# Gathered rows of a mixture-of-experts kernel as fp16 halves, transposed by DMA instead of on TensorE

## The reference, cut to what matters

```python
x = x + tanh(g_xattn) * xattn(layernorm(x), ctx, Wq, Wkv_expand, Wout)
xf = layernorm(x)                              # 2048 tokens x 512
scores = softmax(xf @ gate_w.T); weights, idx = top_k(scores, 2)
h = einsum('td,eid->eti', xf, w1)              # 512 -> 256, each expert
g = silu(h) * einsum('td,eid->eti', xf, w3)
eo = einsum('eti,edi->etd', g, w2)             # 256 -> 512
y = sum over the two chosen experts of weight * eo
z = silu(xf @ ws1.T) * (xf @ ws3.T) @ ws2.T    # shared expert
out = x + tanh(g_ffn) * (y + z)
```

## Time and profile before

| | |
|---|---|
| median of 3 runs | 523.39 us (520.7 to 524.97) |
| the profiled execution | 525.32 us |
| its span in the profile | 523.5 us |
| mean granted TensorE clock | 0.947 |
| batches, to the first gather | 0 to 316.7 us |
| tiles of the experts | 316.7 to 523.5 us |

### The profile page before, as it was taken

One profiled execution on the slowest core, in us unless ns is written; L12 is line 12 of the kernel. 1 busy time (PEld: TensorE's weight loads), 2 busy tenths in 40 slices (PEclk: granted clock), 3 DMA queues, 4 the chain that ended last, 5 costly groups with the idle time before them and its releaser, 6 DMA issues. The chain is left out here.

```text
span 523.5 us, 8113 instructions
## 1 busy us (share of the span) xinstructions
PE 435.4 (83%) x2432; PEld 233.2 (45%) x2433; DVE 322.2 (62%) x641; ACT 246.0 (47%) x425; POOL 240.2 (46%) x185
## 2 busy tenths in 40 slices
PE   2699699988999889987756723999999999999991
PEld 1355455554555545544323311454555455455540
DVE  4798768887588865898888952343434343434330
ACT  4877554563356534486733611333433444333430
POOL 4008235405544154466583633255455455555532
PEclk9999789999999999999895975999999999999996
DMA  8970001120011100325649554166666665756652
GB/s 310 418 307 1 0 1 41 41 81 2 1 60 42 60 0 0 117 105 180 242 121 258 131 113 112 30 108 115 120 104 104 114 120 87 123 112 104 121 75 42
DMA packets 26375, 55.31 MB, mean 106 GB/s; under 512 B 9136, under 2 KB 9264, under 8 KB 25712
## 3 DMA queue, kind: packets, MB, share of 16 engines
q0 software_dynamic: 9760, 20.49, 22.2%
q1 hardware_dynamic: 16592, 34.54, 20.3%
HBM read 31.51 MB, written 23.50 MB: 105 GB/s over the span
## 5 line engine op out<-in xcount | busy, mean ns | idle before, releaser
L1288 PE MATMUL bank<-arena 128*128 128x512 f16 (+1 forms) x576 | 111.0, 350 | 3.2 <-issue 1.5
L1288 PE MATMUL bank<-arena,GT 128*128 x468 | 109.2, 384 | 0.2 <-issue 0.2
L521 POOL DMA_INDIRECT out<-Y,entry x39 | 61.6, 1579 | 84.0 <-ACT Y L787 41.1
L1288 PE MATMUL bank<-arena,gT 128*128 (+1 forms) x330 | 81.3, 383 | 5.4 <-DVE gT L810 4.9
L1288 PEld LDWEIGHTS bank<-arena 128*128 128x128 f16 x576 | 56.3, 99 | 52.6 <-issue 5.8
L536 ACT ACTIVATE arena<-bank 128x512 f16<-128x512 f32 (+1 forms) x88 | 49.8, 586 | 50.9 <-PE bank L1288 31.3
L1288 PEld LDWEIGHTS bank<-arena,GT 128*128 128x128 f16 x468 | 46.3, 99 | 48.3 <-issue 2.9
L810 DVE TENSOR_TENSOR GT<-bank,GT 128x512 f16<-128x512 f32 x39 | 27.0, 692 | 61.0 <-ACT GT L536 61.0
L452 POOL TENSOR_TENSOR arena<-arena,rd 128x1024 f32<-128x1024 f32 x16 | 30.5, 1905 | 52.3 <-DVE rd L923 52.3
L1288 PEld LDWEIGHTS bank<-arena,gT 128*128 128x128 f16 x330 | 32.1, 98 | 42.3 <-DVE gT L810 4.6
L1252 DVE SCALAR_TENSOR_TENSOR uu<-th,bank 128x256 f32<-128x256 f32 x39 | 16.4, 421 | 55.8 <-ACT th L772 55.8
(11 more groups left out here) (126 smaller groups left out, 602.2 us busy)
## 6 DMA issues: line engine op xcount, KB each, us to landing
x_sb<-in_experts SPq DMA_DIRECT2D x16, 768.0 KB, 6.0
xrows<-xn SPq DMA_DIRECT2D x16, 256.0 KB, 2.1
out<-x_sb SPq DMA_DIRECT2D x16, 256.0 KB, 2.2
xrows<-Y SPq DMA_DIRECT2D x1, 2304.0 KB, 24.5
out<-Y SPq DMA_DIRECT2D x1, 2304.0 KB, 28.6
x_sb<-in_x SPq DMA_DIRECT2D x2, 1024.0 KB, 9.1
x_sb<-in_x SPq DMA_DIRECT2D x1, 2048.0 KB, 16.4
arena<-in_wq SPq DMA_DIRECT2D x1, 1024.0 KB, 9.3
```

What stands on the lines that cost most here:

```text
L521: nc.gpsimd.indirect_dma_start(out=out, out_offset=bass.IndirectOffsetOnAxis(ap=entry[:, j, 0:1], axis=0), in_=Y[:, j % RING, :], in_offse ...
L1288: last = nc.tensor.matmul(dst, a, b, start=n == 0, stop=n == len(steps) - 1)
```

## The change

`xrows` holds each row as 1024 fp16: 512 high halves and 512 low halves (the same 2 KB). `row_half` makes them before the store: the high one on ACT, the low one on POOL for the batches 0 to 2 and on DVE for the last. Both lie in `xnh`, in the space of `Y` and a part of `G`. The gathered tile of 128 x 1024 fp16 is transposed from `G` to `GT` by one DMA that SP issues (`dma_start_transpose`); the four PE transposes and the `rows_hi` and `rows_lo` of each tile are gone. Gathers run up to five tiles ahead, PE makes the hidden products two tiles ahead, and `gT` has three buffers. The router's and the shared expert's input of the batches is still turned on PE.

```diff
-        xrows = nc.dram_tensor("xrows", (ROWS, D), F32)
+        xrows = nc.dram_tensor("xrows", (ROWS, 2 * D), F16)
...
             def store_rows(b):
                 for i in range(PER):
-                    sp.wait_ge(xn2_ready, 4 * b + i + 1)
+                    sp.wait_ge(row_lo, 4 * b + i + 1)
...
             load_pieces(0, 2)
+            store_rows(B - 2)
             store_base(B - 2, 0, 1)
             load_pieces(2, 4)
             store_base(B - 2, 1, PER)
             sp.wait_ge(st_base, 16 * PER * (B - 1))
-            load_pieces(4, 12)
+            load_pieces(4, 15)
             store_rows(B - 1)
-            load_pieces(12, 15)
...
-            for j in range(TILES):
+            def turn_rows(j):
+                s = j % RING
+                sp.wait_ge(ld_rows[s], 16 * (j // RING + 1))
+                if j >= RING:
+                    sp.wait_ge(eh_mm, j - RING + 1)
+                sp.dma_start_transpose(GT[:, s].rearrange("p h c t -> p (h c) t"), G[:, s]).then_inc(e_turned[s], 16)
+
+            def watch(j):
+
                 sp.wait_ge(added[j % RING], 16 * (j // RING + 1))
                 sp.sem_inc(landed, 1)
                 if j + AHEAD < TILES:
                     load_list(j + AHEAD)
+
+            for j in range(RING):
+                turn_rows(j)
+            for j in range(TILES):
+                if j + RING < TILES:
+                    turn_rows(j + RING)
+                if j > 0:
+                    watch(j - 1)
+            watch(TILES - 1)
...
                     softmax_mul(b, i)
+                    if prev is not None and i > 1:
+                        row_half(prev, 2 * (i - 2))
+                        row_half(prev, 2 * (i - 2) + 1)
...
+            def gather_after(j):
+                pool.wait_ge(e_turned[j % RING], 16 * (j // RING))
+                gather(j)
...
             for j in range(TILES):
-                if j + RING + 1 < TILES:
-                    pool.wait_ge(eT_mm, j + 2)
-                    gather(j + RING + 1)
+                if j + RING + 2 < TILES:
+                    gather_after(j + RING + 2)
                 add_rows(j)
...
-            def hidden_e(j, s, e):
-                pe.wait_ge(eT_lo, j + 1)
+            def hidden_e(j, s, it, e):
+                pe.wait_ge(e_turned[s], 16 * (it + 1))
...
+            def step(it, s, two=True, one=True):
+
+                j = RING * it + s
+                e = expert_of(j)
+                if two:
+                    hidden_e(j + 2, (s + 2) % RING, it + (s + 2) // RING, expert_of(j + 2))
+                if one:
+                    turn_g_e(j + 1, (s + 1) % RING)
                 pe.wait_ge(egT_lo, j + 1)
```

More of the change, by code:

```diff
@@ L215, in block_program @@
         added = [sem(f"added{n}") for n in range(RING)]
[L216 removed]
+        e_turned = [sem(f"e_turned{n}") for n in range(RING)]
         eh_mm, eth_ready, eu_ready, eg_ready = sem("eh_mm"), sem("eth_ready"), sem("eu_ready"), sem("eg_ready")
@@ L598, in exps, with row_half @@
                 nc.scalar.activation(si, si, ACT.Exp, scale=float(HD) ** -0.5 / (S_Q * S_KV)).then_inc(exp_ready, 1)
+            def row_half(b, i):
+                act.wait_ge(xn2_ready, 4 * b + i + 1)
+                act.wait_ge(st_init, 48)
+                if not isinstance(b, int) or b > 0:
+                    act.wait_ge(st_rows, 64 * b)
+                hi(xnh[:, i, 0, :], xn2[:, i * D:(i + 1) * D]).then_inc(row_hi, 1)
             def tanh_h(b, i):
@@ L637, in feed_forward @@
                 exps(c, 3)
+                row_half(f, 0)
+                row_half(f, 1)
                 if nxt:
@@ L643, in feed_forward @@
                 fill_v(c, (2, 3))
+                row_half(f, 2)
+                row_half(f, 3)
                 between(0)
@@ L677, in last_feed_forward @@
                 turn_hi(c, "g", 0)
+                for i in range(PER):
+                    row_half(f, i)
                 split_piece(10)
@@ L800, in _ @@
             for s in range(RING):
-                step(ROUNDS - 1, s, turn=s == 0, nxt=s < 2)
+                step(ROUNDS - 1, s, two=s == 0, one=s < 2)
         @block.vector
@@ L1557, in step @@
                 turn(e_g, gg[:, s, :], IC).then_inc(egT_mm, 1)
-                if isinstance(j, int) and j == 0:
-                    for k in range(PIECES - 4, PIECES):
-                        pe.wait_ge(w_split[w_slot(k)], w_round(k))
-                if nxt:
-                    hidden_e(j + 1, (s + 1) % RING, e_next)
+            def step(it, s, two=True, one=True):
+                j = RING * it + s
+                e = expert_of(j)
+                if two:
+                    hidden_e(j + 2, (s + 2) % RING, it + (s + 2) // RING, expert_of(j + 2))
+                if one:
+                    turn_g_e(j + 1, (s + 1) % RING)
                 pe.wait_ge(egT_lo, j + 1)
@@ L1575, in _ @@
                 pe.wait_ge(w_split[w_slot(k)], w_round(k) - 1 + (e + 2) // E)
-            hidden_e(0, 0, e)
+            hidden_e(0, 0, 0, e)
+            for k in range(PIECES - 4, PIECES):
+                pe.wait_ge(w_split[w_slot(k)], w_round(k))
+            hidden_e(1, 1, 0, expert_of(1))
             pe.wait_ge(base_ready, NT)
+            turn_g_e(0, 0)
             for s in range(RING):
@@ L1583, in _ @@
             for s in range(RING):
-                step(ROUNDS - 1, s, turn_=s == 0, nxt=s < 2)
+                step(ROUNDS - 1, s, two=s == 0, one=s < 2)
 def kernel(**inputs):
```

95 lines of the change are left out of this document (44 added, 51 removed).

## The result

The changed kernel takes 599.83 us (median of 4, 597.1 to 604.9) beside 523.71 for the kernel before: ratio 1.144, 95% interval 1.139 to 1.150. The forecast was 548.4, range 523 to 582. The direction was right; the time lies above the range.

What follows compares the result with a forecast made beforehand. PE bounds the tiles before; afterwards a loop through SP was to. With a transpose landing L of 4.2 us, 13 L - 29.7, including 8 us for the batches, gave +25 us: 548.4 us against the median, range 523 to 582.

Steps and rivals of the forecast that it cites:

- The loop through SP: Tiles: SP's in-order queue puts each transpose behind an earlier tile's add; three steps take 11.6 us plus the transpose's landing time.
- PE's step of 4.10: Tiles: without the 0.49 us turn of the rows, PE's own step falls from 4.59 to 4.10 us.
- E(0): Start of the tiles: the end of the first down product, at 332.6 us plus the transpose's landing time.
- L = 4.2: Tiles: time from a transpose's issue to its landing, taken from the gather's 4.2 us, bounds 2.1 and 6.0.
- PE stays at the full clock: Tiles: PE, busy for 12.3 of 15.8 us, keeps its clock; 13 slow groups of twelve matmuls would add 23 us.
- rival C: Tiles: transposes land in 6 us or more (572 us), or PE's clock falls (571 us); chance 0.20.
- One add in each turn: Tiles: the wait of an expert's first tile for the add before it, about 2 us, cancelled by another correction.
- Batches, +8: Making the row halves in the batches: 2 us in two loop iterations, 5.3 last iteration, 0.5 last feed-forward; bounds 0 and 14.
- The last iteration's +5.3: Last batch iteration: piece 2 loads behind batch 2's stores, so PE's next product starts near 257.5 instead of 252.25 us.
- A: Transpose lands like a plain store, 2.1 us, and the batches cover the halves: 513.0 us; chance 0.10.
- B: Transpose lands at plain speed, 2.1 to 2.9 us, and the batches pay 8 us: 526.2 us; chance 0.17.
- D: Tiles: SP's wait isn't the last, PE stays the bound at 4.10 us a step: about 514 us; chance 0.02.

Runs made afterwards that it cites:

- the clock mostly back (0.96): Changed kernel with two waits rewritten, plus four unused PE products before each hidden product: 598.6 us, ratio 1.145.
- the loop opened: Changed kernel with two waits rewritten, and SP's wait for the add one tile later, or two: 559.1 us (1.065) and 562.3 us (1.076).
- One execution (538.7 us): Fastest of four executions of the changed kernel with SP's add wait one tile later and two unused PE products per step; median 551.8 us.

## Why the prediction was wrong in size and right in sign

The measured time is 51 us above the forecast: 41 in the tiles (233.0 for the 38 steps instead of 192.4) and 10 in the batches (18.2 instead of 8). The loop through SP was right as a mechanism. What failed were three of its terms, and the price of the halves.

- **PE's step of 4.10**: right. It is seen wherever nothing else holds PE, in the changed kernel too (441.16 and 445.26 are the starts of two hidden products in a row).
- **The loop through SP, three steps = 11.6 + L**: right in its place and its links; opening it gave 43.5 us. Also right: E(0), the first down, some 20.5 us after the first gather (20.1 by the working).
- **L = 4.2**: mis-sized. The chain of the changed kernel goes round with 11 transposes, 57.5 us together, 5.2 each; the slow ones take 6.1 to 7.4. The row that I took for it, the gather, is a mean over positions, while the transpose on the chain often starts with a gather. I had written that it "begins when POOL's next gather does", and gave that no price of its own. The shortest possible, 3.0, is already above the plain store's 2.1.
- **PE stays at the full clock**: wrong. I had the priced alternative (23 us) only in rival C and argued against it from PE's busy share of 12.3 in 15.8 us. The trace has 16 stops in the tiles instead of 13. Behind eleven of them, of 2.0 to 7.0 us, the granted clock was 0.5 for all or a part of the twelve matmuls, the lower level, and they took 3.9 to 5.1 us instead of 2.6. Behind the five of 1.1 to 1.8 us they took 2.6. It cost 21.7 us of PE time, some 19 of them on the chain (eleven groups of twelve with 49.7 us, where 2.75 each make 30.3).
- **One add in each turn**: undersized. The waits of an expert's first tile, "off the path" before, come onto it: the chain has 14 adds for 11 transposes. I had priced them at 2 us and let them cancel.

By the chain's entries between 357 and 590 us, against twelve turns as forecast: PE 67.2 instead of 52.0 (+15), adds 69.5 instead of 58.8 (+11), transposes 57.5 instead of 50.4 (+7), ACT, POOL, SP and issue 38.8 instead of 31.2 (+8). These do not add up as if independent: with the clock mostly back (0.96) the transposes on the chain became 6.2 us, and the time hardly fell. Rival C named both causes as alternatives; they came together. A slow transpose is not needed for a stop that is long enough: behind the two on the chain that landed in 3.15 and 3.05 us, PE had stopped for 2.6 and 2.0 us, and its twelve matmuls took 4.45.

- **Batches, +8**: undersized, 18.2. One us for each loop iteration was 5.5 (3 to 6 over the nine kernels with this code), since I priced POOL's operation by its own engine's spare time and not by what it does to DVE. The last iteration's +5.3 came out as +5.8 (2.8 to 5.9) for a wrong reason: not piece 2 behind the stores (putting the stores later gave nothing) but the same halves. The last feed-forward's 0.5 was 3.1, and it stays without the other halves (56.3 against 52.6). The halves of batch 3 may be its cause; no run took them away.
- **Rivals A, B and D** fell: L of 3.0 at best, and no cover in the batches.
- **Missing altogether**: the load of the DMA engines. At 4.2 to 4.3 us of work for each tile they stand just above PE's 4.10. In the traces with the loop opened and the sum kept, the shares of 0.81 to 0.89 went with steps of 4.9 to 5.1, above the 4.67 of before, so in the mean the 19 us that a shorter PE step could give were not to be had even without the loop. One execution (538.7 us) shows that this is no hard limit.

On the rules weighed: "as fast as regular DMAs" (the Trainium skill, Advanced Engine Details and Errata, X-Bar Transpose (TRN2)) does not hold for this form in time to landing: 3.0 us at best and 3.4 in the median, against 2.0 for a plain store of the same 256 KB in the same run. The estimate of 2.6 us was too low as well, since no transpose landed in under 3.0. The fit behind it (the Trainium skill, DMA: Bandwidth & Descriptors, Anatomy of one DMA) is one for DMAs issued by GpSimd, while SP issues these. The 1309 ns for each 128x128 block (the Trainium skill, VectorE: DVE Perf Modes, The three transpose paths) does not sum over the eight blocks of one DMA either, since all eight land in 3.0.

Open: why a transpose beside a gather takes 4 to 9 us. The runs show the company and the load of the engines, not the mechanism between them.

## What to carry to other kernels

Before moving work from the bounding engine to the DMA engines, work out share times step for them as for any engine, and add the new transfer's packets; 2.9 busy us in a step of 4.67 looked like room for more, and there was little once 1.3 to 1.8 us were added and everything came in bursts. When a transfer is put into an in-order queue behind a wait, follow the loop it closes, and price its links by what else starts at that very moment, here a gather, and with the clock that PE has after the pause. An elementwise operation on an engine that is half idle is not free if it holds up the engine that feeds the bottleneck; moving it to that engine gave nothing either.

## What the runs showed of the hardware

- SP needs 1.23 to 1.53 us (median 1.26, changed kernel) to issue one DMA transpose of 128 x 1024 fp16, against 0.34 for a list load.
- Such a transpose goes in 1024 packets of 256 B and takes 1.3 to 1.8 us of all 16 DMA engines. In the changed kernel it lands in 3.1 to 3.2 us with an add issued in the same moment, and in 4.4 to 7.4 with a gather issued within 0.9 us; with the loop opened, in up to 9.0.
- An accumulating scatter of 256 KB lands in some 5 us (medians of 4.9 to 5.1 where the landing of all 39 is known), a plain one in 2.9. With the plain one a tile needs 1.3 us less of the DMA engines (3.0 against 4.3).
- In the changed kernel's tiles, behind stops of 2.0 to 7.0 us twelve matmuls took 3.9 to 5.1 us; behind stops of 1.1 to 1.8 us they took 2.6, as without a stop. This is no fixed border: with four added products in each step one stop of 3.65 us left them at 2.6.
- While POOL ran two operations of 1.15 us on SBUF, two DVE products that take 0.28 us together took 2.25.
